# Layer norm moments moved from the second layer of a four-layer graph network into the first: even pairs in advance, odd pairs in halves

## The reference

```python
h = jnp.maximum(_layernorm(x, axis=-1), 0.0)
x = x + _L0_gnn_ref(h, adj, Wq, Wk, Wv)        # masked q.k, divided by its row norm, times v
h = jnp.maximum(_layernorm(x, axis=-1), 0.0)
x = x + _L1_gnn_ref(h, W, a, beta, adj)        # graph attention
h = jnp.maximum(_layernorm(x, axis=-1), 0.0)
x = x + _L2_gnn_ref(h, adj, weight, bias)      # graph convolution
h = jnp.maximum(_layernorm(x, axis=-1), 0.0)
x = x + _L3_gnn_ref(h, adj, Wq, bq, Wk, bk, Wv, bv, Wo, bo)   # 8-head attention
```

```python
h = jnp.einsum('bnc,cf->bnf', x, W)
s1 = jnp.einsum('bnf,f->bn', h, a1); s2 = jnp.einsum('bnf,f->bn', h, a2)
e = jax.nn.leaky_relu(s1[:, :, None] + s2[:, None, :], negative_slope=ALPHA)
e = e * mask[None, :, :]
att = jax.nn.softmax(e, axis=2)
h_prime = jnp.einsum('bij,bjf->bif', att, h)
return jax.nn.elu(h_prime + beta * h)
```

## Time and profile before

| | |
|---|---|
| runs | 754.49, 755.95 and 757.42 us, median 755.95 |
| the profiled execution | 755.72 us, its span 753.8 us |
| busy in the span | PE 709.9, PEld 657.7, DVE 627.1, ACT 564.8, POOL 474.5 us |
| first layer's steps | from about 22 to 181 us |
| second layer | from 180.75 us (first product) to about 329 us |
| third and fourth layer | from 329 and from about 399 us to the end |

### The profile page before, as it was taken

How to read it: one execution, slowest core, us unless ns; L and a number is a source line. 1 busy time by engine, 2 the same in 40 slices (tenths; PEclk the granted TensorE clock), 3 DMA queues, 4 the chain that set the end, 5 groups by cost and what they waited for, 6 DMA issues and landing times.

```text
span 753.8 us, 22983 instructions
## 1 busy us (share of the span) xinstructions
PE 709.9 (94%) x6938; PEld 657.7 (87%) x6938; DVE 627.1 (83%) x2650; ACT 564.8 (75%) x1896; POOL 474.5 (63%) x610
## 2 busy tenths in 40 slices
PE   6999999998999999779998999999999999999995
PEld 5999999997777777679997899999999999999984
DVE  5888778776899999869998888888888888888863
ACT  3665655653778787747663899999999999999985
POOL 2445445445678778478884766667666766667652
PEclk9999999999999999879999999999999999999999
DMA  7323300000000000000000000000000000000001
GB/s 233 86 84 86 96 14 0 0 0 1 2 0 2 1 2 0 2 1 0 0 0 1 3 29 28 28 28 14 28 28 28 28 15 28 28 28 28 14 30 43
DMA packets 21682, 20.15 MB, mean 27 GB/s; under 512 B 2432, under 2 KB 21632, under 8 KB 21632
## 3 DMA queue, kind: packets, MB, share of 16 engines
q1 hardware_dynamic: 19440, 18.16, 7.6%
q10 hardware_dynamic: 2192, 1.44, 0.7%
HBM read 11.21 MB, written 8.39 MB: 26 GB/s over the span
## 4 chain that ended last, share of the span: by engine, by line
PE 76%; DVE 16%; issue 4%; ACT 1%; POOL 1%; DMA 1%; DVEq 0%; POOLq 0%; ACTq 0%
PE bank L253 43%; PE bank L1083 7%; PE bank L1075 5%; PE bank L1093 4%; PE bank L323 4%; PE bank L153 4%; PE bank L233 3%; PE bank L333 3%; DVE stats L116 3%; DVE xs L854 2%; DVE masked_e L830 2%; DVE leaky_e L835 2%; DVE att L848 2%; DVE small L838 2%; PE bank L243 1%
## 5 line engine op out<-in xcount | busy, mean ns | idle before, releaser
L1152 ACT ACTIVATE prob<-wide,small 128x128 f32<-128x128 f32 x512 | 199.0, 395 | 20.0 <-DVE small L1236 20.0
L1201 POOL TENSOR_TENSOR prob<-prob,small 128x512 f32<-128x512 f32 x128 | 133.3, 1041 | 104.3 <-DVE small L1250 104.3
L142 POOL TENSOR_TENSOR rstd<-vare,mhalf 128x2 f32<-128x2 f32 x128 | 88.8, 694 | 64.9 <-DVE vare L131 64.9
L1236 DVE CUSTOM_DVE_ANT_0 wide<-bank,mbias 128x128 f32<-128x128 f32 x512 | 116.0, 283 | 9.3 <-PE bank L1075 9.3
L224 POOL TENSOR_SCALAR xn<-xs,nmean,rstd 128x256 f32<-128x256 f32 x186 | 102.4, 561 | 12.8 <-POOL rstd L142 10.8
L116 DVE BATCH_NORM_STATS2 stats<-xs 128x6 f32<-128x256 f32 (+1 forms) x256 | 95.5, 415 | 5.8 <-DMA xs<-in_x_dram 4.7
L1152 ACT ACTIVATION_READ_ACCUMULATOR prob<-wide,small 128x1 f32 x512 | 98.4, 192 | 0.0
L1159 ACT COPY probT<-bank 128x512 f32<-128x512 f32 x128 | 72.1, 588 | 6.3 <-PE bank L1083 5.3
L1083 PE MATMUL bank<-ident,prob 128*128 128x128 f32 x512 | 73.9, 276 | 1.9 <-POOL prob L1201 1.9
L490 POOL TENSOR_TENSOR rnorm<-norm,mhalf 128x2 f32<-128x2 f32 x32 | 22.1, 691 | 79.9 <-ACT relsq L431 79.9
L1083 PEld LDWEIGHTS bank<-ident,prob 128*128 128x128 f32 x512 | 57.0, 140 | 8.9 <-issue 5.9
(11 more groups left out here) (136 smaller groups left out, 1795.9 us busy)
## 6 DMA issues: line engine op xcount, KB each, us to landing
out_dram<-xs SPq DMA_DIRECT2D x32, 256.0 KB, 2.1
xs<-in_x_dram SPq DMA_DIRECT2D x29, 256.0 KB, 2.7
xs<-in_x_dram ACTq DMA_DIRECT2D x1, 512.0 KB, 7.2
xs<-in_x_dram ACTq DMA_DIRECT2D x1, 256.0 KB, 4.0
wq<-in_L_gnn_Wq_dram SPq DMA_DIRECT2D x1, 256.0 KB, 3.6
wk<-in_L_gnn_Wk_dram ACTq DMA_DIRECT2D x1, 256.0 KB, 4.9
wv<-in_L_gnn_Wv_dram SPq DMA_DIRECT2D x1, 256.0 KB, 5.5
w<-in_L_gnn_W_dram SPq DMA_DIRECT2D x1, 256.0 KB, 7.3
```

What stands on the lines that cost most here:

```text
L142: nc.gpsimd.tensor_tensor(rstd[:, b, :], vare[:, b, :], mhalf[:, :], ALU.pow).then_inc(rstd_ready, 1)
L1152: ins = nc.scalar.activation(prob[:, r, i, :], wide[:, r, i, :], ACT.Exp, bias=nmax[r][:, i:i + 1], scale=-1.0, accum_out=rsum[r][:, i:i + 1])
L1201: nc.gpsimd.tensor_tensor(prob[:, r, :, :], prob[:, r, :, :], rinv[r].unsqueeze(2).to_broadcast([128, QUAD, N]), ALU.mult).then_inc(prob_r ...
L1236: nc.vector.tensor_tensor_reduce(out=wide[:, r, i, :], in0=SS[r][:, i * N:(i + 1) * N], in1=mbias[:, :], scale=-1.0, scalar=3e38, op0=ALU. ...
```

## The change

The second layer's moments of pair 2k are now taken in the first layer, in step 2k + 1, right after that pair's update (`moments_even`); `nmean_even` and `vare_even` are written for four pairs (8 columns) at a time, and POOL makes their roots with one instruction for 8 columns (`root_even`), three times within the first layer and once at its end. In the second layer POOL's steps for even pairs have no root of their own any more (`centre_first`). The moments of odd pair 2i + 1 are spread over two of the second layer's steps (`moments_odd`): the first graph's `bn_stats` in one, the second graph's and all the rest in the next. The first layer's loop on DVE is written out instead of a hardware loop. The core of the diff (left out are five declarations of semaphores and names, and two places where `mhalf` is now sliced):

```diff
@@ -58,7 +58,12 @@
         bq = sb("bq", [128, C])
         bk = sb("bk", [128, C])
 
-        mhalf = sb("mhalf", [128, 2])
+        mhalf = sb("mhalf", [128, 8])
+        stats_even = sb("stats_even", [128, 2, 6])
+        mv_even = sb("mv_even", [128, PAIRS // 2, 2, 2])
+        vare_even = sb("vare_even", [128, PAIRS])
+        nmean_even = sb("nmean_even", [128, PAIRS])
+        rstd_even = sb("rstd_even", [128, PAIRS])
         stats = sb("stats", [128, 2, 2, 6])
         mv = sb("mv", [128, 2, 2, 2])
         vare = sb("vare", [128, 2, 2])
...
@@ -224,6 +230,63 @@
                 ins = nc.gpsimd.tensor_scalar(xnb[b][:, g, :], x_of(p, g), nmean[:, b, g:g + 1],
                                               rstd[:, b, g:g + 1], ALU.add, ALU.mult)
             ins.then_inc(xn_ready, 1)
+
+        def root_even(pool, q):
+
+            pool.wait_ge(l1_even_stats, q + 1)
+            part = slice(8 * q, 8 * q + 8)
+            nc.gpsimd.tensor_tensor(rstd_even[:, part], vare_even[:, part], mhalf[:, :], ALU.pow).then_inc(l1_even_root, 1)
+
+        def centre_first(pool, p, turned, freed):
+
+            if p % 2:
+                b = (p // 2) % 2
+                inverse_root(pool, p // 2, l1_stats_ready, l1_rstd_ready, b)
+                pool.wait_ge(l1_rstd_ready, p // 2 + 1)
+                scalars = [(nmean[:, b, g:g + 1], rstd[:, b, g:g + 1]) for g in range(2)]
+            else:
+                pool.wait_ge(l1_even_root, p // 8 + 1)
+                scalars = [(nmean_even[:, p + g:p + g + 1], rstd_even[:, p + g:p + g + 1]) for g in range(2)]
+            pool.wait_ge(turned, freed)
+            for g in range(2):
+                ins = nc.gpsimd.tensor_scalar(xnb[p % 2][:, g, :], x_of(p, g), *scalars[g], ALU.add, ALU.mult)
+            ins.then_inc(l1_xn_ready, 1)
+
+        def moments_even(dve, k):
+
+            dve.wait_ge(l0_x_done, 2 * k + 1)
+            if k > 0:
+                dve.wait_ge(l1_even_step, 2 * k)
+            for g in range(2):
+                ins = nc.vector.bn_stats(stats_even[:, g, :], x_of(2 * k, g))
+            ins.then_inc(l1_even_step, 1)
+            dve.wait_ge(l1_even_step, 2 * k + 1)
+            for g in range(2):
+                ins = nc.vector.bn_aggr(mv_even[:, k, g, :], stats_even[:, g, :])
+            ins.then_inc(l1_even_step, 1)
+            if k % 4 == 3:
+                q, pairs = k // 4, slice(k - 3, k + 1)
+                dve.wait_ge(l1_even_step, 2 * k + 2)
+                mean, var = (mv_even[:, pairs, :, i].rearrange("p k g -> p (k g)") for i in range(2))
+                part = slice(8 * q, 8 * q + 8)
+                nc.vector.scalar_tensor_tensor(nmean_even[:, part], mean, -2.0, mean, ALU.mult, ALU.add)
+                nc.vector.scalar_tensor_tensor(vare_even[:, part], var, EPS, var, ALU.add, ALU.max).then_inc(l1_even_stats, 1)
+
+        def moments_odd(dve, i, g):
+
+            b = i % 2
+            if g == 0 and i < 2:
+                dve.wait_ge(l0_xn_ready, PAIRS - 1 + i)
+            elif g == 0:
+                dve.wait_ge(l1_xn_ready, 2 * i - 2)
+            ins = nc.vector.bn_stats(stats[:, b, g, :], x_of(2 * i + 1, g))
+            if g == 1:
+                ins.then_inc(l1_step, 1)
+                dve.wait_ge(l1_step, 2 * i + 1)
+                for g in range(2):
+                    ins = nc.vector.bn_aggr(mv[:, b, g, :], stats[:, b, g, :])
+                ins.then_inc(l1_step, 1)
+                root_argument(dve, i, l1_step, l1_stats_ready, b)
 
         def gather_nodes(pe, ps, p, src, xn_ready):
 
...
@@ -511,12 +574,13 @@
 
                 for p in range(1, PAIRS - 2):
                     step(p, p % 2)
+                    if p % 8 == 1 and p > 1:
+                        root_even(pool, p // 8 - 1)
                 for n in range(2):
-                    inverse_root(pool, n, l1_stats_ready, l1_rstd_ready, n)
                     inverse_norm(PAIRS - 3 + n)
-                    pool.wait_ge(tr_done, PAIRS - 1 + n)
-                    centre(pool, n, n, l1_rstd_ready, l1_xn_ready)
+                    centre_first(pool, n, tr_done, PAIRS - 1 + n)
                 inverse_norm(PAIRS - 1)
+                root_even(pool, PAIRS // 8 - 1)
 
             @block.vector
             def _(dve):
@@ -642,9 +706,12 @@
                         constants()
                     if p > 1:
                         weight_low(p - 2)
-                with dve.Fori(3, PAIRS // 2 - 2) as j:
-                    step(2 * j + 1, 1)
-                    step(2 * j + 2, 0)
+                    if p % 2:
+                        moments_even(dve, p // 2)
+                for p in range(7, PAIRS - 3):
+                    step(p, p % 2)
+                    if p % 2:
+                        moments_even(dve, p // 2)
                 for n, p in enumerate(range(PAIRS - 3, PAIRS)):
                     if p + 1 < PAIRS:
                         low_part(p + 1, (p + 1) % 2)
@@ -652,12 +719,13 @@
                     mask(p, p % 2)
                     update(p - 1)
                     low_v(p)
-                    if n < 2:
-                        dve.wait_ge(xn_ready, p + 2)
-                        layer_norm_stats(dve, n, l1_step, l1_stats_ready, n)
+                    if n != 1:
+                        moments_even(dve, p // 2)
+                    else:
+                        moments_odd(dve, 0, 0)
+                        moments_odd(dve, 0, 1)
                 relation_low(PAIRS - 1)
-                dve.wait_ge(l1_xn_ready, 1)
-                layer_norm_stats(dve, 2, l1_step, l1_stats_ready)
+                moments_odd(dve, 1, 0)
                 update(PAIRS - 1)
 
 
@@ -809,9 +877,7 @@
 
                 for p in range(PAIRS + 1):
                     if p + 2 < PAIRS:
-                        inverse_root(pool, p + 2, stats_ready, rstd_ready, p % 2)
-                        pool.wait_ge(tr_done, p + 1)
-                        centre(pool, p + 2, p % 2, l1_rstd_ready, l1_xn_ready)
+                        centre_first(pool, p + 2, tr_done, p + 1)
                     else:
                         root_and_shift(pool, p + 2 - PAIRS, l2_stats_ready, l2_rstd_ready, l2_shift_ready, p % 2)
                     if p >= 4:
@@ -855,17 +921,20 @@
                                                    ALU.max, ALU.add).then_inc(x_done, 1)
 
                 def step(p):
-                    ahead, step_sem, ready_sem, freed, when = p + 3, dstep, stats_ready, xn_ready, p + 2
-                    if p + 3 >= PAIRS:
-                        ahead, step_sem, ready_sem = p + 3 - PAIRS, l2_step, l2_stats_ready
-                        if ahead == 2:
-                            freed, when = l2_xn_ready, 1
                     if p >= 1:
                         mask_max(p - 1)
-                    dve.wait_ge(freed, when)
-                    moments(dve, ahead, step_sem, (p + 1) % 2)
-                    mean_variance(dve, ahead, step_sem, (p + 1) % 2)
-                    root_argument(dve, ahead, step_sem, ready_sem, (p + 1) % 2)
+                    if p + 3 < PAIRS:
+                        if p % 2 == 0:
+                            moments_odd(dve, p // 2 + 1, 1)
+                        elif p + 4 < PAIRS:
+                            moments_odd(dve, p // 2 + 2, 0)
+                    else:
+                        ahead = p + 3 - PAIRS
+                        if ahead < 2:
+                            dve.wait_ge(l1_xn_ready, PAIRS - 2 + 2 * ahead)
+                        else:
+                            dve.wait_ge(l2_xn_ready, 1)
+                        layer_norm_stats(dve, ahead, l2_step, l2_stats_ready, ahead % 2)
                     if p >= 1:
                         inverse(p - 1)
                         attention(p - 1)
```

More of the change, by code:

```diff
@@ L141, in inverse_root @@
             pool.wait_ge(stats_ready, p + 1)
-            nc.gpsimd.tensor_tensor(rstd[:, b, :], vare[:, b, :], mhalf[:, :], ALU.pow).then_inc(rstd_ready, 1)
+            nc.gpsimd.tensor_tensor(rstd[:, b, :], vare[:, b, :], mhalf[:, 0:2], ALU.pow).then_inc(rstd_ready, 1)
         def root_and_shift(pool, p, stats_ready, rstd_ready, shift_ready, b=0):
@@ L177, in gnn_stack_kernel @@
         out_done, x_done, dstep = sem("l0_out_done"), sem("l0_x_done"), sem("l0_dve_step")
-        l0_x_done = x_done
+        l0_x_done, l0_xn_ready = x_done, xn_ready
         w_high, v_high, relm_high, relm_low = sem("l0_w_high"), sem("l0_v_high"), sem("l0_relm_high"), sem("l0_relm_low")
@@ L204, in gnn_stack_kernel @@
         l1_xn_ready, l1_tr_done, l1_hT_ready, l1_step = sem("l1_xn_ready"), sem("l1_tr_done"), sem("l1_hT_ready"), sem("l1_dve_step")
+        l1_even_step, l1_even_stats, l1_even_root = sem("l1_even_step"), sem("l1_even_stats"), sem("l1_even_root")
         l2_stats_ready, l2_rstd_ready, l2_shift_ready = sem("l2_stats_ready"), sem("l2_rstd_ready"), sem("l2_shift_ready")
@@ L489, in inverse_norm @@
                     pool.wait_ge(x_done, since(p))
```

(2 more changed lines are left out.)

## The result

The changed kernel takes 765.16 us (median of 5 runs, 764.51 to 766.16) where the kernel before takes 755.95: ratio 1.0128, interval 1.0112 to 1.0145. It is slower by 9.2 us by the medians and by 9.7 by the ratio. The profiled execution has a span of 764.0 us for 753.8: the second layer's first product is 1.87 us later, the layer itself 7.56 longer, and the other 0.8 lies in the third and fourth layer, which the change doesn't touch (425.58 us for 424.81, with a mean clock of 0.98 for 0.99).

What follows compares the result with a forecast made beforehand. DVE's chain was taken to set the second layer's pace, 4.05 us a step. 755.7 + 10.5 (meetings with POOL) + 1.2 (passage) + 0.3 (first layer) = 767.7, given as 767 us; range 752.5 to 772.

Steps and rivals of the forecast that it cites:

- the first case: Second layer: POOL's `add` or centring gets ahead of `att` or `leaky_e` every two steps; 762 to 773 us, chance 0.57.
- the alternative: Second layer's odd step: `leaky_e` loses its 0.14 us lead over POOL's `add`; 1.1 less 0.4, +0.7 us.
- The step laid out in full: Second layer's even step: `att` waits for the centring, then for POOL's `add`; +1.35 us, about +1.0 per two steps.
- the number taken: Second layer: likeliest loss from meetings, 0.95 us per two steps, 11 times, +10.5 us.
- the floor: Second layer: shortest step, 3.82 us, by PE's and ACT's chain; 3.88 was taken, for a gain of 4.1 us.
- The passage: Between first and second layer: moments ahead of the last `relation_low` delay `outputs` and the first product; +1.2 us, bound +1.9.
- the 1.5: The passage's +1.2 and the first layer's +0.3 us, as added to the meetings' cost in the cases.
- the third case: Second layer: no meeting of DVE and POOL matters; 753.1 us, 750.4 at the low end, chance 0.23.
- The first layer: Added moments make `rels` late in steps 3 and 5, +0.3 us; root of eight columns 0, bounds 0 and 0.5.
- its rule: DVE and POOL in SBUF: whoever issues first holds the shared ports for its whole instruction, the other fully blocked.

Runs made afterwards that it cites:

- x_hold: Changed kernel, with POOL's `add` waiting for `leaky_e` in the second layer's odd steps (5 to 29): 755.54 us, ratio 0.9998 to the kernel before.
- x_onestep: Changed kernel, with an odd pair's moments whole in the second layer's even steps, none in odd ones: 757.89 us, ratio 1.0039 to the kernel before.
- x_before_late: Kernel before, with two needless reciprocals on DVE in each second-layer step, behind `vare` and ahead of `leaky_e`: 783.97 us, ratio 1.0373.
- x_hold_passage: Changed kernel, `add` waiting for `leaky_e` in odd steps, pair 30's moments behind the last `relation_low`, pair 3's behind the last update: 751.09 us, again 752.33.
- x_before_less: Kernel before, with one `bn_stats` less in each second-layer step (second graph's moments left out): 759.11 us, ratio 1.0032.

## Why the prediction was right, and where it wasn't

**Slower, by a meeting of DVE and POOL in every two steps: right.** 765.2 stands beside 767, within the first case. x_hold, x_onestep and x_before_late show the cause from three sides: they take the meeting away, move the two instructions apart, and bring the meeting about in the kernel before.

**Which meeting: wrong in the main, right in the alternative.** The step laid out in full, `att` behind centring and `add` in the even step (+1.35), didn't happen: `att` keeps 0.35 us. The `leaky_e` of the step with the root loses its lead, as the prediction's last sentences on the matter had it, and so DVE falls 1 us behind POOL; the even step's centring (240.98 to 242.25) is over when `att` comes (242.88). The layout had added a second meeting to a phase that the first one rules out. Where the first is removed, `att` does meet the centring, and that costs 0.08 to 0.24; the block by the `add` behind it (+1.35 in all) came in no run.

**The size.** For two steps the alternative gave +0.7, and the number taken was +0.95, 11 times. The two periods from reciprocal to reciprocal are 3.80 (242.68 to 246.48) and 4.83, together 0.53 more than 2 x 4.05, and 11 such pairs of steps lie between the first and the last `leaky_e` of 1.46 us or more (213.95 and 308.83). So the count came out and the term of one pair was too large; over the layer it is +7.0 where +10.5 was summed. The blocked `leaky_e` costs 1.46 - 0.42 = 1.04, near the 1.1 taken, and the step without a meeting ran at the floor (3.80 for 3.82) and not at the 3.88 taken.

**The passage: mis-sized.** +1.2 was taken, with bounds to 1.9; it is +2.5 at the first `masked_e`, of which 0.23 came along from the first layer. The order of DVE's work is 1.22, as summed. The product takes 3.81, as the upper bound had it (twice 1.90), which brings 0.63 by the first `masked_e`. What no term had is the low clock on `outputs`: 1.35 for 0.94, another 0.42 at the product's start. The +1.2 taken left the clock out altogether.

**Luck in the number.** The two errors have opposite signs: 3.5 too much in the steps and 1 too little in the passage. They left 767 nearer than its terms deserve; with the steps sized rightly and the passage as taken the sum would have been about 764. Two ends of cases don't follow from their terms, and nothing rests on them: 11 x 1.3 and the 1.5 give 771.5, and only the upper bounds of passage and first layer (1.9 and 0.5) come near 773; the third case's 750.4 is 751.4 by its terms (755.7 - 5.5 + 1.2).

**The first layer: right.** The last update but one starts at 177.04 for 176.81: +0.23, with +0.3 predicted. The root of eight columns takes 1.64 us, between its bounds of 0.69 and 2.8, and is hidden.

**Not settled.** x_hold_passage runs 3.94 us per step in its steady part (3.97 in the mean of the layer) where 3.8 was seen in single steps. What is left of the meetings there is 0.21 on `leaky_e` and 0.09 on `att` (0.70 for 0.61) in two steps. They trade places when the hold is widened, and no run took away both. The one row that the prediction had against its rule, the second `att` after 197.27 that kept its time though a centring had begun 0.10 before it, wasn't taken up by any run. Why the clock between the layers falls in one execution and not in another is open as well.

## What to carry to other kernels

When a change shortens one engine's work, write down the start times of the other engine's instructions beside it, not only the chain that gets shorter: here a lead of 0.14 us decided 1.04 us per step. A group's mean or its median alone hides this; the least and the most of the durations give it away. And a wait put on the engine that isn't the bottleneck (POOL's `add` behind `leaky_e`) is worth trying before any rearrangement; it turned a loss of 1.3% into none.

## What the runs showed of the hardware

- `leaky_e` (both inputs in SBUF) against the `add`, no semaphore between them: with a lead of 0.14 us it takes 0.44, with one of 0.05 it takes 0.42 (x_before_less), level with it 1.55 (x_before_late), 0.09 behind 1.46 (the changed kernel), 0.92 behind 0.63 (x_hold). In each of the last three it ends 0.28 or 0.29 us after the `add` ends, wherever it began: the blocked instruction pays what is left of the other one. The loser can be either engine: beside a `leaky_e` that came first, the `add` takes 1.44 to 1.52 for 1.27.
- How small a lead decides: in x_before_less leads of 0.04 and 0.05 us were always enough. At 0.03 by the recorded starts it was won twice and lost once, and in x_before_late 0.01 lost:

```profile
273.01 1.59 DVE L835 SCALAR_TENSOR_TENSOR leaky_e<-masked_e 128x256 f32<-128x256 f32 x1
273.04 1.27 POOL L808 TENSOR_TENSOR xs<-xs,exp_u 128x512 f32<-128x512 f32 x1
```

  The Trainium skill (SBUF — State Buffer, "Who interferes with whom") says that whoever issues first has the ports for its whole instruction. These rows agree for leads of 0.04 us and more; below that the recorded start doesn't tell who was first.
- So engines don't wait for each other only at semaphores, as the first section of this document has it: here DVE and POOL also wait for each other where the program has no semaphore between them.
- The executions of one kernel differ by their clock. Of the runs of the kernel before on one chip, those with a mean granted clock of 0.993 have spans of 751.5 to 751.9 us, those with 0.986 755.2 to 755.8 (five and three of them). Between the layers the clock falls in one execution and stays in the next: x_hold_passage had 1.00 from 182 to 185 us and its first reciprocal at 188.1, the same kernel in its second set of runs 0.58 and 189.9. A single profile of such a passage is one draw.
